# Keys turned for the outer products by a transposing DMA instead of TensorE, in a linear-attention and decision-tree layer on one core

## The chip, the cores and the metric

One core of a Trainium2 chip runs the whole layer. The metric is the device time of one execution in microseconds (us), lower is better. The kernel is written instruction by instruction for five engines that run at the same time and meet only at semaphores: TensorE (PE, with its weight loads as PEld), VectorE (DVE), ScalarE (ACT), GpSimd (POOL) and the queue that issues DMAs (SP). Each engine takes its instructions in the order in which they are written.

## The reference, cut to what matters

x is 4 x 2048 x 256 in float32. It is normalised by row (xn), and two branches are added to x:

```
Q = elu(xn @ Wq + bq) + 1      K = elu(xn @ Wk + bk) + 1      V = xn @ Wv + bv      # 16 heads of 64
KV[t] = KV[t-1] + K[t]^T V[t]          Ks[t] = Ks[t-1] + K[t]                       # causal, per head
attn  = (Q[t] KV[t]) / (Q[t] . Ks[t] + 1e-6) @ Wo + bo
gate  = sigmoid((xn @ tree_Wq^T) @ routers^T)                 # 255 nodes of a binary tree of depth 8
leaf  = product of gate or 1 - gate along each of 256 paths
out   = x + attn + (leaf @ leaf_values) @ Wout^T + Wout_b
```

## The kernel before

The 8192 tokens are 16 blocks of 512. In a block the 16 heads are taken two at a time, so a block has 8 units, p = 0 to 7, and the kernel 128 (n = 8 g + p). A unit takes its pair of heads in 8 chunks of 64 tokens: the products inside a chunk go through a masked matrix of scores, what came before goes through a running sum of outer products K^T V, kept as `snaps` (one after each chunk) and `state` (from block to block). V has a column of ones, which gives the denominator.

Precision comes from split operands: a float32 operand is held as a high part and a low part of TensorE's fast type, and a product is three passes (high by high, high by low, low by high). A projection of 256 inputs is therefore 6 matmuls of 512 columns. The high part is a copy by ScalarE (`high`, `high_of_output`), the low part a subtraction by VectorE (`low`, `low_of_output`).

PSUM is eight banks: two for outer products, and six that are filled and drained by turns, W0 and W1 (`w_pair`), S0 and S1 (`s_pair`), O0 and O1 (`o_pair`). A "fill" is a group of matmuls into one of the six; its drain frees the bank. S0 and S1 also hold the scores, O0 and O1 the outputs.

One unit n on TensorE:
- `tiled(n)`: the outputs of unit n from the state (`from_state`), the outer products of unit n + 1 (`outer_products_when_ready`; they need the keys by tokens, `k_tok`), the scores of unit n + 1 (`scores_when_ready`), the outputs of unit n from its masked scores (`from_chunk`). The scores wait until the queries of unit n + 1 are drained, and until S0 and S1 are: S1's last fill is the unit's "tail".
- the fills of `unit_fills(g, p)` (line 27), in that order: a head in W1 (V1 at p = 0, a transposed xn (`xT`) of the next block at p = 1, 2, transposed leaves at 3, 4, gates at 5, 6), the keys of unit n + 2 in W0, the queries of unit n + 2 in S0, the tail in S1 (a quarter of the values, at p = 0 to 6), the keys of unit n + 2 turned (`kT`, line 702: four 128x128 transposes, features by tokens into tokens by features), and the outputs of unit n turned (`oT`, line 709). At p = 7 there are the two halves of the block's result, `y`, instead of head and tail (60 matmuls each), and `kT` stands between them.

The other engines follow the same list. ScalarE (line 470): `copy_scores(n + 1)`, then by kind: `exponential` for K and Q (a Relu, line 407, and an Exp, line 410, on 128x512), `high` for xT and leaf, Tanh for gates, `copy_keys` for kT (line 420, PSUM to `k_tok`), `high_of_output` for oT (line 430). VectorE (line 617): `carry(n + 1)`, seven or eight dependent sums of outer products (line 585), `norm(n)`, then by kind: `phi` for K and Q (line 520), `low`, `values` (line 529), `low_of_output` (line 544). At p = 2 and 6 `values_first` puts the values ahead of the queries' phi. GpSimd (line 371): the mask of unit n + 1 (line 329), at p = 1 the residual (line 337), at p = 7 the eight levels of the next block's tree (lines 345 to 362), at p = 0 the inverse deviation. SP (line 284): the load of x two blocks ahead, and the two stores of a block's result.

`kT` and `qT` have two buffers each, by p % 2; `k_tok` has one.

Of the kernel before, what the change touches and what calls it, by code (L numbers as in the profile page):

```python
# [7 lines left out]
F32 = mybir.dt.float32  # L8
F32R = mybir.dt.float32r

P = 128
# [15 lines left out]
def unit_fills(g, p, blocks):  # L27

    n = g * PAIRS + p
    ahead = divmod(n + 2, PAIRS) if n + 2 < blocks * PAIRS else None  # L30
    more = g + 1 < blocks
    head, tail = [], []
    if p == 0:
        head, tail = [("V1", 0, g)], [("V1", 1, g)]
    if p in (1, 2):
        tail = [("V1", p + 1, g)]
        if more:
            head = [("xT", p - 1, g + 1)]
    if p in (3, 4):
        head = [("leaf", p - 3, g)]  # L40
        if more:
            tail = [("V0", p - 3, g + 1)]
    if p in (5, 6) and more:
        head, tail = [("gate", p - 5, g + 1)], [("V0", p - 3, g + 1)]

    fills = [(name, W1) for name in head]
    if ahead:
        fills += [(("K", ahead[1], ahead[0]), W0), (("Q", ahead[1], ahead[0]), S0)]
    fills += [(name, S1) for name in tail]
    if p == PAIRS - 1:  # L50

        fills += [(("oT", p, g), W1), (("y", 0, g), O1)]
    if ahead:
        fills.append((("kT", ahead[1], ahead[0]), W0))
    fills.append((("y", 1, g), S1) if p == PAIRS - 1 else (("oT", p, g), W1))
    return fills
# [4 lines left out]
         (("gate", 0, 0), S0), (("gate", 1, 0), S1), (("kT", 0, 0), W0), (("K", 1, 0), W0), (("Q", 1, 0), W1),  # L61
         (("kT", 1, 0), W0)]


def attention_and_tree_layer(nc, x, Wq, bq, Wk, bk, Wv, bv, Wo, bo,
# [45 lines left out]
    with ExitStack() as ctx:  # L111
        def sb(name, shape, dt=F32):
            return ctx.enter_context(nc.sbuf_tensor(name, shape, dt))

        def sem(name):
            return ctx.enter_context(nc.semaphore(name))
# [66 lines left out]
        tree_cols = [xn[:, 0:2].rearrange("p c n -> p (c n)"), xn[:, 2:4].rearrange("p c n -> p (c n)"),  # L183
                     k_tok[:, :, :].rearrange("p c n -> p (c n)")]
        leafvT, woutT, routersT = [t.rearrange("p (t n) -> p t n", t=2) for t in tree_cols]
# [39 lines left out]
        a_masked = sem("a_masked")  # L225
        kv_filled = sem("kv_filled")
        sum_ready = sem("sum_ready")
        o_begun = sem("o_begun")
# [28 lines left out]
        def _(sp):  # L257
# [25 lines left out]

            for g in range(BLOCKS):
                if g + 2 < BLOCKS:
                    sp.wait_ge(x_consumed, g + 1)
                    sp.dma_start(x_in[:, g % 2], x_rows[g + 2]).then_inc(x_loaded[g % 2], 16)
                for i in range(2):
                    name = ("y", i, g)
                    sp.wait_ge(drained[bank_of[name]], count_of[name])  # L290
                    sp.dma_start(out_rows[g, :, 2 * i:2 * i + 2, :],
                                 y_buf[:, 2 * i:2 * i + 2, :]).then_inc(y_stored, 16)
            sp.wait_ge(y_stored, 32 * BLOCKS)

        @block.gpsimd
        def _(pool):
# [67 lines left out]
            FIRST_LEVELS = {0: range(0, 5), 1: range(5, 7), 2: range(7, depth)}  # L364

            mask(0)
            gates(0)
            pool.wait_ge(leaf_step, 1)  # L370
            for n in range(UNITS):
                g, p = divmod(n, PAIRS)
                if p == 0 and g + 1 < BLOCKS:
                    inverse_deviation(g + 1)
                    pool.wait_ge(rstd_ready, 2 * g + 4)
                if n + 1 < UNITS:
                    mask(n + 1)
                if p == 1:
# [12 lines left out]
        @block.scalar  # L391
        def _(act):
# [25 lines left out]
            def copy_keys(name):  # L418
                act.wait_ge(filled[bank_of[name]], count_of[name])
                act.activation(k_tok[:, :, :].rearrange("p c n -> p (c n)"), psum_of(name), ACT.Copy)\  # L420
                   .then_inc(drained[bank_of[name]], 1)

            def high_of_output(name):
# [43 lines left out]
            exponential(("Q", 1, 0))  # L467
            copy_keys(("kT", 1, 0))

            for n in range(UNITS):  # L470
                if n + 1 < UNITS:
                    copy_scores(n + 1)
                for name, _ in unit_fills(n // PAIRS, n % PAIRS, BLOCKS):
                    kind, i, g = name
                    if kind in "KQ":
                        exponential(name)
                    elif kind == "oT":
                        high_of_output(name)
                    elif kind == "kT":
                        copy_keys(name)  # L480
                    elif kind == "xT":
                        high(name, xnT[:, g % 2, 0, i])
                    elif kind == "leaf":
                        high(name, leafT[:, 0, i])
                    elif kind == "gate":
                        half_gates(name)

        @block.vector
        def _(dve):
# [25 lines left out]
            def phi(name):  # L515
                kind, p, _ = name
                slot, dst = (0, kT) if kind == "K" else (1, qT)
                col = p + (PAIRS if kind == "K" else 0)
                dve.wait_ge(exp_ready, exp_count[name])
                dve.scalar_tensor_tensor(out=dst[:, p % 2], in0=psum_of(name), scalar=bias_one[:, col:col + 1],  # L520
                                         in1=ex[:, slot], op0=ALU.add, op1=ALU.max)\
                   .then_inc(drained[bank_of[name]], 1)
# [91 lines left out]
            carry(0)  # L614
            phi(("Q", 1, 0))

            for n in range(UNITS):
# [25 lines left out]
        def _(pe):  # L643
# [7 lines left out]

            def split_product(dst, lhs, rhs, tiles):
                steps = [s for t in range(tiles) for s in passes(lambda a, t=t: lhs(a, t), lambda a, t=t: rhs(a, t))]
                for i, (l, r) in enumerate(steps):
                    last = pe.matmul(dst, l, r, start=i == 0, stop=i == len(steps) - 1)  # L655
                return last
# [15 lines left out]

            def fill(name):
                kind, i, g = name
# [3 lines left out]
                if kind in "KQ":  # L678
                    wt = wk if kind == "K" else wq
                    last = split_product(dst, lambda a, t: wt[:, a, t, i * P:(i + 1) * P],  # L680
                                         lambda a, t: xnT[:, g % 2, a, t], KT_)
                elif kind in ("V0", "V1"):
                    half, n = int(kind[1]), 2 * HALF * D
                    last = split_product(dst, lambda a, t: xnT[:, g % 2, a, t, i * P:(i + 1) * P],
                                         lambda a, t: wv[:, a, t, half * n:(half + 1) * n], KT_)
                elif kind in ("xT", "leaf"):
# [13 lines left out]
                elif kind == "kT":  # L700
                    for c in range(CH):
                        last = pe.transpose(dst[:, c * P:(c + 1) * P], kT[:, i % 2, c * P:(c + 1) * P], ident[:, :])  # L702
# [172 lines left out]
            until_drained(("K", 1, 0))  # L875
            fill(("kT", 1, 0))
            until(split_lo_pool, len(LO_POOL))
            until(split_lo, len(LO_VECTOR))

            for n in range(UNITS):  # L880
                tiled(n)
                fills = unit_fills(n // PAIRS, n % PAIRS, BLOCKS)

                first_by_vector = fills[0][0][0] in ("V1", "xT", "leaf")
                for name, bank in fills:
# [15 lines left out]
                    if kind == "kT":  # L901
                        until_drained(("K", i, g))
                    fill(name)

# [24 lines left out]
```

## Time and profile before

| | |
|---|---|
| median of 3 runs | 1276.48 us (1273.93 to 1276.64) |
| the profiled execution | 1273.15 us, of which the trace's span is 1271.4 us |
| TensorE busy | 1244.6 us, 98% of the span (weight loads, beside it, 1105.0) |
| VectorE | 810.3 us, 64% |
| ScalarE | 622.4 us, 49% |
| GpSimd | 374.3 us, 29% |
| granted TensorE clock | 0.997 of full speed (2.4 GHz) |
| DMA | 25.91 MB in 21597 packets, 20 GB/s on average |

In the profile a line such as `676.80 0.75 DVE L520 ...` is an instruction (or a run of like ones, x6) with its start and its duration in us, the engine, the line of the kernel, the tile written, the tiles read and the shape; in brackets is how long the engine had been idle and what released it. TensorE's instructions overlap: the pitch from the start of one group to the start of the next is what a group costs, and the duration of one is longer than its share.

### The profile page before, as it was taken

How to read it: one execution, taken by the hardware profiler on the slowest of the kernel's cores; microseconds unless marked ns; L12 is line 12 of the kernel's file. 1: busy time of each engine (PE TensorE's matmuls, PEld its weight loads, DVE VectorE, ACT ScalarE, POOL GpSimd, SP SyncE). 2: the span in 40 equal slices, each digit the busy share in tenths (PEclk: the TensorE clock that was granted, in tenths of full speed). 3: DMA queues.
4: the chain of work that ended last, by engine and by line, in shares of the span. 5: the costliest groups of instructions: out<-in, count | busy, mean ns of one | idle time of the engine just before them, and what ended most of it. 6: DMA issues, size and time to landing. Idle time of an engine off the chain costs nothing.

```text
span 1271.4 us, 48688 instructions
## 1 busy us (share of the span) xinstructions
PE 1244.6 (98%) x22173; PEld 1105.0 (87%) x22173; DVE 810.3 (64%) x2186; ACT 622.4 (49%) x1007; POOL 374.3 (29%) x590
## 2 busy tenths in 40 slices
PE   5899999999999999999999999999999999999997
PEld 5789888898988989889898988989889898898986
DVE  4675766757576574765757666575765758657473
ACT  4563654536446363653636445364553636536361
POOL 3424232132421413223142321324214132231320
PEclk9899999999999999999999999999999999999999
DMA  6000001000000000001000010000000000000000
GB/s 223 19 3 19 19 2 35 3 18 20 10 28 3 19 19 10 28 3 36 2 19 19 3 35 3 19 20 10 28 3 19 19 18 20 2 19 3 19 3 18
DMA packets 21597, 25.91 MB, mean 20 GB/s; under 512 B 1025, under 2 KB 19728, under 8 KB 21392
## 3 DMA queue, kind: packets, MB, share of 16 engines
q1 hardware_dynamic: 21392, 22.82, 5.5%
q8 instruction: 173, 2.83, 0.9%
q14 instruction: 32, 0.26, 0.1%
HBM read 14.43 MB, written 8.39 MB: 18 GB/s over the span
## 4 chain that ended last, share of the span: by engine, by line
PE 97%; DVE 1%; ACT 1%; DMA 1%; SPq 0%; issue 0%; DVEq 0%
PE s_pair L655 25%; PE w_pair L655 20%; PE o_pair L667 9%; PE s_pair L667 9%; PE o_pair L765 6%; PE kv_pair L740 5%; PE o_pair L779 5%; PE s_pair L729 5%; PE w_pair L709 4%; PE w_pair L702 4%; PE w_pair L689 3%; DMA ffn_tok<-in_L_ffn_Wout_w_dram 1%; DVE snaps L585 0%; SPq L267 0%; PE o_pair L655 0%; ACT ex L407 0%
## 5 line engine op out<-in xcount | busy, mean ns | idle before, releaser
L329 POOL TENSOR_SCALAR_AFFINE_SELECT aT<-aT 64x512 f32<-64x512 f32 x256 | 167.6, 655 | 833.0 <-ACT aT L434 824.7
L655 PE MATMUL w_pair<-xnT,wk 128*128 128x512 f32 x768 | 205.7, 403 | 0.7 <-ACT k_tok L420 0.7
L655 PE MATMUL s_pair<-xnT,wq 128*128 128x512 f32 x756 | 194.0, 392 | 0.0
L434 ACT ACTIVATE aT<-s_pair 128x512 f32<-128x512 f32 x128 | 76.4, 597 | 238.3 <-PE s_pair L729 238.3
L585 DVE TENSOR_TENSOR snaps<-kv_pair,snaps 128x65 f32<-128x65 f32 x768 | 173.3, 226 | 26.4
L520 DVE SCALAR_TENSOR_TENSOR kT<-w_pair,bias_one,ex 128x512 f32<-128x512 f32 x128 | 96.2, 751 | 122.7 <-ACT ex L410 122.6
L655 PEld LDWEIGHTS s_pair<-xnT,wq 128*128 128x128 f32 x756 | 142.1, 188 | 31.4
L655 PE MATMUL s_pair<-wv,xnT 128*128 128x512 f32 x648 | 168.7, 395 | 0.0
L410 ACT ACTIVATE ex<-ex 128x512 f32<-128x512 f32 x256 | 161.8, 632 | 8.1
L407 ACT ACTIVATE ex<-w_pair,neg_bias 128x512 f32<-128x512 f32 x130 | 89.5, 689 | 148.5 <-PE w_pair L655 148.5
L655 PEld LDWEIGHTS w_pair<-xnT,wk 128*128 128x128 f32 x768 | 136.1, 188 | 26.6 <-ACT k_tok L420 1.0
L655 PEld LDWEIGHTS s_pair<-wv,xnT 128*128 128x128 f32 x648 | 121.6, 188 | 28.6
L420 ACT ACTIVATE k_tok<-w_pair 128x512 f32<-128x512 f32 x128 | 76.4, 597 | 143.0 <-PE w_pair L702 143.0
L520 DVE SCALAR_TENSOR_TENSOR qT<-s_pair,bias_one,ex 128x512 f32<-128x512 f32 x126 | 94.3, 748 | 59.6 <-ACT ex L410 59.6
L765 PE MATMUL o_pair<-snaps,qT 64*64 64x65 f32 x3584 | 112.2, 225 | 3.5 <-DVE state L585 3.5
L544 DVE TENSOR_TENSOR oT<-w_pair,oT 128x512 fp32r<-128x512 f32 x128 | 88.3, 690 | 27.4 <-ACT oT L430 27.4
L667 PE MATMUL o_pair<-wo,oT 128*128 128x256 f32 x768 | 94.7, 279 | 0.0
L667 PE MATMUL s_pair<-wo,oT 128*128 128x256 f32 x768 | 94.7, 279 | 0.0
L667 PEld LDWEIGHTS o_pair<-wo,oT 128*128 128x128 f32 x768 | 91.9, 188 | 0.0
L667 PEld LDWEIGHTS s_pair<-wo,oT 128*128 128x128 f32 x768 | 91.9, 188 | 0.0
L562 DVE TENSOR_TENSOR o_tok<-o_pair,rden 128x512 f32<-128x512 f32 x128 | 88.5, 691 | 4.4
L765 PEld LDWEIGHTS o_pair<-snaps,qT 64*64 64x64 f32 x3584 | 83.6, 135 | 8.7 <-issue 8.4
(105 smaller groups left out, 1953.7 us busy)
## 6 DMA issues: line engine op xcount, KB each, us to landing
x_in<-in_L_attn_x_dram SPq DMA_DIRECT2D x16, 512.0 KB, 3.9
out_dram<-y_buf SPq DMA_DIRECT2D x32, 256.0 KB, 2.1
stage<-in_L_attn_Wv_dram SPq DMA_DIRECT2D x2, 512.0 KB, 8.0
stage<-in_L_attn_Wk_dram SPq DMA_DIRECT2D x2, 512.0 KB, 9.6
stage<-in_L_attn_Wq_dram SPq DMA_DIRECT2D x2, 512.0 KB, 10.8
stage<-in_L_attn_Wo_dram SPq DMA_DIRECT2D x2, 512.0 KB, 9.1
bv_all<-in_L_attn_bv_dram SPq DMA_DIRECT2D x1, 512.0 KB, 8.6
ffn_tok<-in_L_ffn_Wq_dram SPq DMA_DIRECT2D x1, 256.0 KB
```

Of the source, the lines that this page charges most:

```text
L329: pool.affine_select(out=part, in_=part, compare_op=ALU.is_ge, fill=0.0, base=0, pattern=[[0, 2 * CH], [1, D]], channel_multiplier=-1).the ...
L407: act.activation(ex[:, slot], psum_of(name), ACT.Relu, scale=-1.0, bias=neg_bias[:, col:col + 1])\
L410: act.activation(ex[:, slot], ex[:, slot], ACT.Exp, scale=-1.0).then_inc(exp_ready, 1)
L420: act.activation(k_tok[:, :, :].rearrange("p c n -> p (c n)"), psum_of(name), ACT.Copy)\
L434: act.activation(aT[:, n % 2].rearrange("p h c q -> p h (c q)"), s_pair[:, :, 0:CH * D], ACT.Copy).then_inc(s_copied, 1)
L520: dve.scalar_tensor_tensor(out=dst[:, p % 2], in0=psum_of(name), scalar=bias_one[:, col:col + 1], in1=ex[:, slot], op0=ALU.add, op1=ALU.max)\
L544: dve.tensor_tensor(oT[:, 1, p], psum_of(name), oT[:, 0, p].bitcast(F32), ALU.subtract)\
L562: dve.tensor_tensor(o_tok[:, :, :, :].rearrange("p b t (h e) -> p b (t h) e", e=D), v[:, :, :, 0:D], rden[:, :, :].unsqueeze(3).to_broadca ...
L585: dve.tensor_tensor(dst, added, so_far, ALU.add).then_inc(sum_ready, 1)
L655: last = pe.matmul(dst, l, r, start=i == 0, stop=i == len(steps) - 1)
L667: last = pe.matmul(dst[:, (c % 2) * hid:(c % 2 + 1) * hid], oT[:, a, t, cols] if t < PAIRS else leafT[:, a, t - PAIRS, cols], wo[:, b, t] ...
L765: last = pe.matmul(output_at(t, h, a), qT[rows_of(h), p % 2, t * P + a * D:t * P + (a + 1) * D], before, start=turn == 0 and half not in b ...
```

## The change

- Order: the keys are filled first in each unit, ahead of the head, and three units ahead (n + 3) instead of two. The queries stay two ahead.
- The fill `kT` and its copy are gone, except for the first two units. In their place, for each unit m from 2 on: GpSimd (`take_apart`) reads the float32 keys as pairs of 16-bit words and writes the words into two planes, `k_planes` (128 x 2 x 512); SP (`turn_keys`) issues one transposing DMA from the planes to `k_turned` (128 x 8 x 128, 16 bits); ScalarE (`put_together`), ahead of the queries' exponential, copies the turned words back interleaved into `k_tok`.
- The waits go with it: the planes are free when the DMA before has landed, `k_turned` when ScalarE has put the previous keys together, `k_tok` when the outer products before have run. On TensorE, `masked` and `whole` wait for GpSimd's mask before the last matmul of the queries' fill, and for the keys put together before the last matmul of the tail.
- SP's order: the two stores of block g come at p = 0 of the next block, ahead of that unit's DMA, and the load of x at p = 2.
- At the end of a unit the order is now `oT`, after the tail; at p = 7, `oT`, then both halves of `y`.

```diff
@@ def unit_fills(g, p, blocks):
-    ahead = divmod(n + 2, PAIRS) if n + 2 < blocks * PAIRS else None
+    keys = divmod(n + 3, PAIRS) if n + 3 < blocks * PAIRS else None
+    queries = divmod(n + 2, PAIRS) if n + 2 < blocks * PAIRS else None
...
-    fills = [(name, W1) for name in head]
-    if ahead:
-        fills += [(("K", ahead[1], ahead[0]), W0), (("Q", ahead[1], ahead[0]), S0)]
+    fills = [(("K", keys[1], keys[0]), W0)] if keys else []
+    fills += [(name, W1) for name in head]
+    if queries:
+        fills.append((("Q", queries[1], queries[0]), S0))
     fills += [(name, S1) for name in tail]
+    fills.append((("oT", p, g), W1))
     if p == PAIRS - 1:
-        fills += [(("oT", p, g), W1), (("y", 0, g), O1)]
-    if ahead:
-        fills.append((("kT", ahead[1], ahead[0]), W0))
-    fills.append((("y", 1, g), S1) if p == PAIRS - 1 else (("oT", p, g), W1))
+        fills += [(("y", 0, g), O1), (("y", 1, g), S1)]
@@ buffers
+        k_planes = sb("k_planes", [P, 2, TOK], U16)
+        k_turned = sb("k_turned", [P, 2 * CH, P], U16)
@@ SP
-            for g in range(BLOCKS):
-                if g + 2 < BLOCKS:
-                    sp.wait_ge(x_consumed, g + 1)
-                    sp.dma_start(x_in[:, g % 2], x_rows[g + 2]).then_inc(x_loaded[g % 2], 16)
+            def turn_keys(m):
+                sp.wait_ge(k_apart, m - 1)
+                if m > 2:
+                    sp.wait_ge(k_whole, m - 2)
+                sp.dma_start_transpose(k_turned[:, :, :], k_planes[:, :, :].rearrange("p s t -> p (s t)"))\
+                  .then_inc(k_turned_in, 16)
...
+            turn_keys(2)
+            for n in range(UNITS):
+                g, p = divmod(n, PAIRS)
+                if p == 0 and g:
+                    store(g - 1)
+                if n + 3 < UNITS:
+                    turn_keys(n + 3)
+                if p == 2 and g + 2 < BLOCKS:
+                    sp.wait_ge(x_consumed, g + 1)
+                    sp.dma_start(x_in[:, g % 2], x_rows[g + 2]).then_inc(x_loaded[g % 2], 16)
@@ GpSimd (after the mask of unit n + 1, for unit n + 3)
+            def take_apart(m):
+                g, p = divmod(m, PAIRS)
+                pool.wait_ge(drained[bank_of["K", p, g]], count_of["K", p, g])
+                if m > 2:
+                    pool.wait_ge(k_turned_in, 16 * (m - 2))
+                pool.tensor_copy(k_planes[:, :, :], kT[:, m % 2].bitcast(U16).rearrange("p (t s) -> p s t", s=2))\
+                    .then_inc(k_apart, 1)
@@ ScalarE (before the queries' exponential)
+            def put_together(m):
+                act.wait_ge(k_turned_in, 16 * (m - 1))
+                act.wait_ge(kv_filled, m)
+                act.activation(k_tok[:, :, :].rearrange("p c f -> p (c f)").bitcast(U16)
+                               .rearrange("p (n s) -> p s n", s=2),
+                               k_turned[:, :, :].rearrange("p (s c) f -> p s (c f)", s=2), ACT.Copy).then_inc(k_whole, 1)
...
                     if kind in "KQ":
+                        if kind == "Q":
+                            put_together(n + 2)
                         exponential(name)
@@ TensorE
-                until_drained(("kT", p, g))
+                if n < 2:
+                    until_drained(("kT", p, g))
+                else:
+                    until(k_whole, n - 1)
...
-                        if c == 1 and g * PAIRS + i + 1 < UNITS:
-                            until(a_masked, 2 * (g * PAIRS + i) + 4)
...
+                def masked():
+                    if n + 1 < UNITS:
+                        until(a_masked, 2 * n + 4)
+                def whole():
+                    if n + 2 < UNITS:
+                        until(k_whole, n + 1)
...
-                    fill(name)
+                    fill(name, masked if kind == "Q" else whole if bank == S1 and kind != "y" else None)
+                    if kind == "y" and i == 0:
+                        whole()
+                masked()
+                whole()
```

## Rows read from the trace of the kernel before

**Rows 1.** The page's chain that ended last: shares of the span by engine

```profile
PE 97%; DVE 1%; ACT 1%; DMA 1%; SPq 0%; issue 0%; DVEq 0%
```

**Rows 2.** Stretches, p = 7, 0, 1: length, then each engine's busy us and count

```profile
641.28:661.19 19.91, 19.91 (x269) 19.15 (x268) 8.35 (x25) 5.08 (x9) 11.06 (x21) 1.00 0.05 15
661.19:669.84 8.65, 8.65 (x158) 7.32 (x157) 6.90 (x20) 3.56 (x6) 1.32 (x2) 1.00 0.09 32
669.84:677.58 7.74, 7.74 (x156) 6.67 (x155) 6.06 (x17) 4.93 (x9) 3.73 (x3) 1.00 0.01 4
```

**Rows 3.** Timeline of the unit p = 1: start, duration, engine, line, what

```profile
670.80 0.13 PEld L729 LDWEIGHTS s_pair<-qT,kT 64*64 64x64 f32 x1
...
671.95 0.66 PE L689 MATMUL w_pair<-ident,xn 128*128 128x128 f32 x4
...
675.41 0.69 ACT L407 ACTIVATE ex<-s_pair,neg_bias 128x512 f32<-128x512 f32 x1
...
676.13 0.63 ACT L410 ACTIVATE ex<-ex 128x512 f32<-128x512 f32 x1
...
676.61 0.60 PE L702 MATMUL w_pair<-ident,kT 128*128 128x128 f32 x4
676.80 0.75 DVE L520 SCALAR_TENSOR_TENSOR qT<-s_pair,bias_one,ex 128x512 f32<-128x512 f32 x1 [0.62 <-ACT ex L410]
...
677.05 0.60 PE L709 MATMUL w_pair<-ident,o_tok 128*128 128x128 f32 x4
...
677.47 0.68 DVE L529 TENSOR_TENSOR v_aug<-s_pair,bv_all 128x512 f32<-128x512 f32 x1
...
678.54 0.13 PEld L729 LDWEIGHTS s_pair<-qT,kT 64*64 64x64 f32 x1
```

**Rows 4.** Timeline of the unit p = 7, whose keys are filled first

```profile
643.39 1.66 PE L655 MATMUL w_pair<-xnT,wk 128*128 128x512 f32 x6
...
645.09 0.69 ACT L407 ACTIVATE ex<-w_pair,neg_bias 128x512 f32<-128x512 f32 x1 [1.43 <-PE w_pair L655]
...
647.19 0.63 ACT L410 ACTIVATE ex<-ex 128x512 f32<-128x512 f32 x1
647.29 2.87 PEld L667 LDWEIGHTS o_pair<-wo,oT 128*128 128x128 f32 x24
...
647.72 0.58 ACT L430 ACTIVATE oT<-w_pair 128x512 fp32r<-128x512 f32 x1
...
648.52 0.68 DVE L544 TENSOR_TENSOR oT<-w_pair,oT 128x512 fp32r<-128x512 f32 x1
```

**Rows 5.** Timeline of the unit p = 6, values ahead of the queries' phi

```profile
632.57 0.13 PEld L765 LDWEIGHTS o_pair<-state,qT 64*64 64x64 f32 x1 [0.17 <-issue]
...
640.51 0.69 DVE L529 TENSOR_TENSOR v_aug<-s_pair,bv_all 128x512 f32<-128x512 f32 x1 [0.64 <-PE s_pair L655]
...
641.12 0.74 DVE L520 SCALAR_TENSOR_TENSOR qT<-s_pair,bias_one,ex 128x512 f32<-128x512 f32 x1
...
642.29 0.56 PEld L729 LDWEIGHTS s_pair<-qT,kT 64*64 64x64 f32 x32
```

**Rows 6.** Groups by line and shape: operations of 1024 columns, busy us, mean ns

```profile
L345 POOL TENSOR_SCALAR ffn_tok<-ffn_tok 128x1024 f32<-128x1024 f32 x16 | 17.6, 1102 | 1.4
...
L396 ACT ACTIVATE wv<-stage 128x1024 fp32r<-128x1024 f32 x2 | 2.1, 1050 | 0.0
```

**Rows 7.** DMA queues (packets, MB, share), then DMA issues (KB each, us to landing)

```profile
q1 hardware_dynamic: 21392, 22.82, 5.5%
...
x_in<-in_L_attn_x_dram SPq DMA_DIRECT2D x16, 512.0 KB, 3.9
out_dram<-y_buf SPq DMA_DIRECT2D x32, 256.0 KB, 2.1
stage<-in_L_attn_Wv_dram SPq DMA_DIRECT2D x2, 512.0 KB, 8.0
...
stage<-in_L_attn_Wq_dram SPq DMA_DIRECT2D x2, 512.0 KB, 10.8
```

More of the change, by code:

```diff
@@ L9 @@
 F32R = mybir.dt.float32r
+U16 = mybir.dt.uint16
 P = 128
@@ L226, in attention_and_tree_layer @@
         kv_filled = sem("kv_filled")
+        k_apart = sem("k_apart")
+        k_turned_in = sem("k_turned_in")
+        k_whole = sem("k_whole")
         sum_ready = sem("sum_ready")
@@ L292, in _ @@
                                  y_buf[:, 2 * i:2 * i + 2, :]).then_inc(y_stored, 16)
+            turn_keys(2)
[8 more added lines that the diff above has]
+                    sp.dma_start(x_in[:, g % 2], x_rows[g + 2]).then_inc(x_loaded[g % 2], 16)
+            store(BLOCKS - 1)
             sp.wait_ge(y_stored, 32 * BLOCKS)
@@ L370, in _ @@
             pool.wait_ge(leaf_step, 1)
+            take_apart(2)
             for n in range(UNITS):
@@ L377, in _ @@
                     mask(n + 1)
+                if n + 3 < UNITS:
+                    take_apart(n + 3)
                 if p == 1:
@@ L468, in _ @@
             copy_keys(("kT", 1, 0))
+            exponential(("K", 2, 0))
             for n in range(UNITS):
@@ L515, in phi @@
             def phi(name):
-                kind, p, _ = name
-                slot, dst = (0, kT) if kind == "K" else (1, qT)
+                kind, p, b = name
+                slot, dst = (0, kT[:, p % 2]) if kind == "K" else (1, qT[:, p % 2])
                 col = p + (PAIRS if kind == "K" else 0)
                 dve.wait_ge(exp_ready, exp_count[name])
-                dve.scalar_tensor_tensor(out=dst[:, p % 2], in0=psum_of(name), scalar=bias_one[:, col:col + 1],
+                dve.scalar_tensor_tensor(out=dst, in0=psum_of(name), scalar=bias_one[:, col:col + 1],
                                          in1=ex[:, slot], op0=ALU.add, op1=ALU.max)\
@@ L615, in _ @@
             phi(("Q", 1, 0))
+            phi(("K", 2, 0))
             for n in range(UNITS):
@@ L650, in until, with split_product @@
                     pe.wait_ge(signal, count)
-            def split_product(dst, lhs, rhs, tiles):
+            def split_product(dst, lhs, rhs, tiles, at_last=None):
                 steps = [s for t in range(tiles) for s in passes(lambda a, t=t: lhs(a, t), lambda a, t=t: rhs(a, t))]
                 for i, (l, r) in enumerate(steps):
+                    if at_last and i == len(steps) - 1:
+                        at_last()
                     last = pe.matmul(dst, l, r, start=i == 0, stop=i == len(steps) - 1)
@@ L671, in output_rows, with fill @@
                 return last
-            def fill(name):
+            def fill(name, at_last=None):
                 kind, i, g = name
@@ L684, in fill @@
                     last = split_product(dst, lambda a, t: xnT[:, g % 2, a, t, i * P:(i + 1) * P],
-                                         lambda a, t: wv[:, a, t, half * n:(half + 1) * n], KT_)
+                                         lambda a, t: wv[:, a, t, half * n:(half + 1) * n], KT_, at_last)
                 elif kind in ("xT", "leaf"):
@@ L701, in fill @@
                     for c in range(CH):
-                        last = pe.transpose(dst[:, c * P:(c + 1) * P], kT[:, i % 2, c * P:(c + 1) * P], ident[:, :])
+                        last = pe.transpose(dst[:, c * P:(c + 1) * P], kT[:, i, c * P:(c + 1) * P], ident[:, :])
                 elif kind == "oT":
                     for c in range(CH):
-                        if c == 1 and g * PAIRS + i + 1 < UNITS:
-                            until(a_masked, 2 * (g * PAIRS + i) + 4)
                         to = dst[:, c * P:(c + 1) * P].rearrange("p (a q) -> p a q", a=2)
@@ L876, in _ @@
             fill(("kT", 1, 0))
+            fill(("K", 2, 0))
             until(split_lo_pool, len(LO_POOL))
@@ L882, in _ @@
                 fills = unit_fills(n // PAIRS, n % PAIRS, BLOCKS)
-                first_by_vector = fills[0][0][0] in ("V1", "xT", "leaf")
+                first_by_vector = any(bank == W1 and name[0] in ("V1", "xT", "leaf") for name, bank in fills)
+                def masked():
[4 more added lines that the diff above has]
+                        until(k_whole, n + 1)
                 for name, bank in fills:
```

14 lines of the change are left out of this document (6 added, 8 removed).

## The prediction

> **What bounds the kernel now.** I read the chain of waits first: 97% of the span is TensorE running its own queue [rows 1]. Next the table by stretches: within a block of eight units TensorE is busy for every microsecond of the unit, whether that is the 19.91 us of p = 7, the 8.65 of p = 0 or the 7.74 of p = 1 and 2, at the full clock, while ScalarE is busy for 4.93 of 7.74 us and VectorE for 6.06 [rows 2]. So TensorE is the bound, but the other two are not idle bystanders. The timeline of the unit p = 1 shows how far behind TensorE they follow [rows 3]: TensorE starts the scores of the next unit at 678.54, and just before it VectorE finished phi of the queries (676.80 + 0.75 = 677.55) and then the values (677.47 + 0.68 = 678.15). The scores need both: the queries as an operand, and both S banks empty. The margin is 0.39 us. That margin decides this case.
>
> **What goes.** Four transposes of the keys per unit. Their price is the pitch from their first record to the first of the next group, 677.05 - 676.61 = 0.44 us [rows 3] (the mean of one record is longer, since records overlap). 126 times 0.44 is 55 us. ScalarE's copy of the turned keys out of PSUM goes as well (0.60 us, off the path). If nothing else became late, this would be the gain.
>
> **What comes, and what it costs.** (1) GpSimd splits the keys into planes, 128x1024 elements. The nearest row is its 128x1024 tensor_scalar, 1.10 us [rows 6]; two-byte elements at a stride could cost double, 2.2; I take 1.1. GpSimd is idle most of a unit; at p = 7 the tree's levels start some 3 us later, 11 us of work in a unit of 20, and nothing waits for them until p = 3. (2) ScalarE puts the halves together, again 1024 elements: its 128x1024 SBUF to SBUF copy takes 1.05 us [rows 6]. From below, a 512-column operation is 0.60; from above I see no reason for more than 1.3. I take 1.05. This stands before the queries' exponential in ScalarE's order. (3) The transposing DMA, 256 KB. No row shows one. From below the plain 256 KB store lands in 2.1 us. From above, the weight loads in a full queue land in 8.0 to 10.8 us [rows 7]. Between them: 21392 packets took 5.5% of 16 engines over 1271.4 us, so 52 ns each; the 512 KB load (1 KB packets, 32 to an engine) lands in 3.9 us, of which packets are 1.7 and 2.2 is fixed. If each of 128 partitions and 8 column blocks makes a packet, 64 come to an engine: 3.3 + 2.2 = 5.5 us, the value that I take.
>
> **Is the DMA hidden?** In unit p = 1 keys are filled first. Counting from the unit's start (669.84), the first fill starts at 2.11 (671.95 [rows 3]); a fill of keys in first place is ready for ScalarE 1.70 later (643.39 to 645.09 [rows 4]), so at 3.81; Relu and Exp take 1.35 (675.41 to 676.76), phi 0.75, ending at 5.95; planes to 7.1; SP issues. Putting together stands 5.55 into the next unit (below), 7.74 us or more later: 13.3. So 6.1 us are there for the DMA, and 5.5 just fits. The store of the output and x's load stand in the same queue, but one transfer per unit of 8 us leaves them room; the store at p = 0 is issued before this unit's keys exist.
>
> The Trainium skill disagrees with itself here. "VectorE: DVE Perf Modes", section "The three transpose paths", gives 1309 ns for a 128x128 block through the crossbar, eight of which would be an estimated 10.5 us and not fit; "DMA: Bandwidth & Descriptors" has 261 GB/s for transposes, an estimated 1.0 us of data for 256 KB, which would fit. No run here shows either yet.
>
> **What is late instead.** Before, ScalarE did the head fill's copy in its idle time ahead of the keys; now it comes behind the keys' exponential, and putting together behind that. Unit p = 1, from its start: keys' Relu 3.81; the next independent operation follows Exp 0.53 after its start (647.19 to 647.72 [rows 4], so operations overlap by 0.1), so at 3.81 + 0.72 + 0.53 = 5.06; the copy of xT, 0.60 with 0.1 overlapped, to 5.55; putting together, 0.95 net, to 6.50. The queries' Relu thus starts at 6.50 where it started at 5.57 (675.41). Exp ends at 7.85, phi runs from 7.89, the values follow 0.67 later (676.80 to 677.47) and end at 9.24. With 0.1 for the signal the next scores start at 9.34. TensorE would be there at 7.30 + 0.96 = 8.26. Before it was 8.70 (678.54). So p = 1 gets longer by 0.64 although TensorE has 0.44 less to do. After the first such unit this repeats, since keys are filled 1.15 us after the scores start, in either order.
> p = 3 and 4 have the same order (a leaf copy in xT's place): +0.64 each. At p = 2 the values precede the queries' phi, which ends at 8.64: scores at 8.74, +0.04.
> p = 5 and 6 are 8.71 long (632.57 to 641.28 [rows 2, 5]): their head, gates, takes about 1 us more, by which the queries come later too. In the old order the scores start 3.13 after the queries' Relu (678.54 - 675.41), so at p = 5, where they start at 9.73, Relu is at 6.60. Now gates' Tanh is at 5.2, putting together at 5.7, the queries at 6.64, and the scores 2.84 later (the values' end, 678.15 - 675.41, and 0.1), at 9.48: -0.25. p = 6: values ready at 7.95 (640.51 - 632.57 = 7.94 [rows 5]), phi 0.61 behind, scores at 9.41 instead of 9.72 (642.29 - 632.57): -0.31.
> p = 0: scores were at 8.65 + 0.96 = 9.61, so the queries' Relu at 6.48. ScalarE has no copy for the head here and is through with putting together at 6.1, so Relu stays where it is, and the scores come at 6.48 + 2.84 = 9.32: -0.29.
> p = 7: the queries wait 0.82 for putting together, so the low half of the last output, which ended at 649.21, ends at 650.03; its first reader is the 22nd of 24 weight loads that start at 647.29 at 0.117 each, 649.74 [rows 4]. A stall of 0.37 against 0.44 saved: -0.07.
> Sum of a block: -0.29 + 0.64 + 0.04 + 0.64 + 0.64 - 0.25 - 0.31 - 0.07 = +1.04; 15 blocks, +15.6. The last block has no values at p = 3 and 4, where the new chain costs 0.95 each, and smaller terms elsewhere: +1.9. At the start the third keys have no unit of lead: fill, exponentials, phi, planes, DMA, putting together are 1.7 + 1.35 + 0.75 + 1.1 + 5.5 + 1.05 = 11.5 us, from 1.4 before the first unit, needed at about 7.5 in it: +2.6. In all +20.1 on the profiled execution's 1273.15 us (span 1271.4 and 1.75 around it). The median is 3.3 above that execution: 1276.48 + 20.1 = 1296.6; rounded down a little for overlaps that I don't see, 1295.
>
> **Rivals.**
> A, the forecast: ScalarE's longer queue before the queries' exponential takes the gain back. 1295, its own range 1280 to 1312. Chance 0.53.
> B, faster: ScalarE has the room. Were putting together as cheap as a 512-column copy (0.60), queries start 0.45 earlier at p = 1 to 4 and p = 7: p = 1, 3, 4 cost +0.19 each, p = 2 gains 0.41, p = 7 0.44, p = 0, 5, 6 about 0.9 together: -1.2 a block, -17 in all with the ends, 1259. It decides below about 0.8 us for that operation. With all of it hidden the limit is -55, 1221. For it: ScalarE is busy for only 4.93 of 7.74 us [rows 2]. Against it: where its work stands, not how much it is, and the 1.05 us row. Chance 0.21.
> C, the ring: landing, putting together (1.05), next issue, landing; a unit can't be shorter than the DMA plus 1.25, since there is one buffer for planes and one for turned halves. It costs from 6.5 us on. At the 8.0 us of the load of Wv units take 9.25: p = 1 to 4 +1.5 each, p = 0 +0.6, p = 5 and 6 +0.54 each, so 7.7 a block, 16 blocks: 1400. Chance 0.17.
> D, the eight blocks go one after another: at the 10.8 us of Wq's load a unit takes 12.05, 27 us more in a block, 1710. Against it: that load waited behind others in its queue. Chance 0.09. (The Trainium skill's 1309 ns a block, in "VectorE: DVE Perf Modes", "The three transpose paths", would mean a rival of this kind.)
>
> **How the numbers follow.** A change under 0.2% (2.6 us) can't be told from none. Faster: B and a thin edge of A, 0.22. Same: where A and B meet, 0.07. Slower: A's rest, C, D, 0.71. The range: a tenth below, from B's faster half, and a tenth above, from C's upper part and D: 1245 to 1375.
>
> **What would show it.** In the profile after: no key transposes on TensorE; at p = 1, 3, 4 units of some 8.4 us with TensorE waiting for VectorE's values before the scores; p = 0, 5, 6 shorter by 0.3; the queries' Relu released by ScalarE itself and not by TensorE; putting together at 1.05 us; the transpose landing in under 6.1 us. Wrong if units 1, 3 and 4 are shorter than 7.7 us, or if ScalarE idles before putting together for a DMA.

## The result and the profile after

The change makes the kernel slower: 1307.59 us median (1304.73 to 1307.94, 4 runs) against 1276.56, a ratio of 1.0235 with a 95% interval of [1.0213, 1.0256]. Forecast were 1295 and a range of 1245 to 1375. The profiled execution took 1307.69 us, its span is 1306.0.

The page of the changed kernel: span, busy time by engine, then the chain that ended last, by engine and by line.

```profile
span 1306.0 us, 48282 instructions
...
PE 1244.0 (95%) x21669; PEld 1059.6 (81%) x21669; DVE 801.0 (61%) x2186; ACT 687.3 (53%) x1007; POOL 504.8 (39%) x716
...
PE 60%; ACT 25%; DVE 9%; issue 5%; DMA 1%; SPq 0%; POOL 0%; DVEq 0%; POOLq 0%
PE w_pair L705 20%; ACT k_tok L464 9%; PE s_pair L717 9%; ACT ex L444 8%; PE s_pair L705 8%; PE s_pair L778 5%; PE o_pair L717 5%; PE o_pair L828 5%; DVE qT L567 5%; ACT ex L447 5%; PE o_pair L814 3%; DVE v_aug L576 3%; PE kv_pair L789 3%; PE w_pair L758 2%; ACT leafT L437 1%
```

Where TensorE had 97% of the chain [rows 1], it has 60%, and ScalarE 25%. The largest of ScalarE's lines there is L464, the interleaving. TensorE's busy sum hardly fell (1244.6 to 1244.0 us), although 504 transposes are gone: without them and without the rest of the change it is 1194.7 (the floor below). The three largest groups of fills (w_pair<-xnT,wk; s_pair<-xnT,wq; s_pair<-wv,xnT) have the same counts as before and 32 us more of busy time, so the sum counts some waiting as work and does not show the loss.

The chain itself, in order of time, through the unit p = 1 (start, length, what):

```profile
686.99 0.53 PE s_pair L778 x30
...
688.05 1.60 PE w_pair L705 x6
689.64 0.02 issue
689.67 0.70 ACT ex L444
690.37 0.02 issue
690.39 0.02 ACT ex L447
690.41 0.51 issue
690.93 0.58 ACT xnT L437
691.51 1.26 ACT k_tok L464
692.77 0.54 ACT ex L444
693.31 0.02 issue
693.33 0.64 ACT ex L447
693.98 0.03 issue
694.00 0.75 DVE qT L567
694.75 0.61 DVE v_aug L576
695.36 0.04 issue
695.40 0.62 PE s_pair L778 x26
```

This is the forecast's queue, link by link: keys' fill, keys' Relu and Exp, the copy of xT, the interleaving, the queries' Relu and Exp, phi of the queries, the values, the scores. Before the change the queries' Relu started at 675.41 [rows 3], 0.04 us after the last matmul of its fill (673.84 + 1.53), with ScalarE done 0.02 us earlier:

```profile
673.84 1.53 PE L655 MATMUL s_pair<-xnT,wq 128*128 128x512 f32 x6
...
674.76 0.63 ACT L410 ACTIVATE ex<-ex 128x512 f32<-128x512 f32 x1
```

There the chain runs through TensorE alone; now the Relu has its fill ready and waits for ScalarE's own queue.

One unit goes another way. At p = 2 the chain leaves the interleaving for TensorE itself, in 15 of the 16 blocks: the last matmul of the tail has the new wait for the keys put together (`whole`).

```profile
700.02 1.27 ACT k_tok L464
701.29 0.04 issue
701.33 0.50 PE s_pair L705
```

The outer products, which read those keys, begin only at 702.62. No run moves this wait nearer to them.

The two new operations that matter, by line over the whole run (ns min/median/max), and the DMA's issue (median us to landing):

```profile
L464 ACT ACTIVATE k_tok<-k_turned x126: 1342/1364/1378, 52.2 to 1273.2; 128x1024 uint16<-128x1024 uint16 x126
```

```profile
L396 POOL COPY k_planes<-kT x126: 1037/1042/1045, 47.9 to 1267.9; 128x1024 uint16<-128x1024 uint16 x126
L296 SPq DMA_TRANSPOSE k_turned<-k_planes x126: 1232/1232/2453, 49.0 to 1269.0; - x126
```

```profile
k_turned<-k_planes SPq DMA_TRANSPOSE x126, 3.1
```

The interleaving takes 1.36 us where 1.05 was forecast. GpSimd's split takes 1.04 (1.1 forecast). The only wait that the profile puts to this DMA is that of the first interleaving, 1.2 us. Rivals C and D are out.

How long is a unit? Medians over the blocks of the time from one `copy_scores` of ScalarE to the next, read from the timelines (the columns on the right are experiments below):

| fills of unit | before | forecast | after | floor, no keys turned | straight copy | GpSimd interleaves |
|---|---|---|---|---|---|---|
| p = 0 | 8.78 | 8.49 | 8.34 | 8.35 | 8.33 | 8.33 |
| p = 1 | 7.74 | 8.38 | 8.50 | 7.33 | 8.24 | 7.38 |
| p = 2 | 7.74 | 7.78 | 7.95 | 7.41 | 7.67 | 7.46 |
| p = 3 | 7.73 | 8.37 | 8.49 | 7.31 | 8.22 | 7.38 |
| p = 4 | 7.74 | 8.38 | 8.51 | 7.33 | 8.25 | 7.39 |
| p = 5 | 8.77 | 8.52 | 8.67 | 8.30 | 8.39 | 8.37 |
| p = 6 | 8.71 | 8.40 | 8.41 | 8.39 | 8.40 | 8.45 |
| p = 7 | 19.83 | 19.76 | 19.97 | 19.37 | 19.70 | 19.36 |
| block | 77.04 | 78.08 | 78.84 | 73.79 | 77.20 | 74.12 |

The sign is as forecast in all units but p = 7, which got longer. A block costs 1.80 us more; over 15 blocks that is 27 of the 31. Of the profiled executions, whose spans differ by 34.6, the one after reaches its first copy of scores 3.7 us later (40.66 against 36.92). That is ahead of the first transposing DMA, and the experiments show that it does not belong to the change.

### The profile page after: what moved, and what is told of

The parts are those of the page before. It is cut to its first block, busy times and chain, and to the rows that moved or that the text cites. A ratio compares the mean times of both kernels' runs of the same rounds, so it can differ in the third digit from the quotient of the medians.

```text
span 1306.0 us, 48282 instructions
## 1 busy us (share of the span) xinstructions
PE 1244.0 (95%) x21669; PEld 1059.6 (81%) x21669; DVE 801.0 (61%) x2186; ACT 687.3 (53%) x1007; POOL 504.8 (39%) x716
## 2 busy tenths in 40 slices
DMA packets 154655, 58.94 MB, mean 45 GB/s; under 512 B 134082, under 2 KB 152785, under 8 KB 154449
## 3 DMA queue, kind: packets, MB, share of 16 engines
q1 hardware_dynamic: 154448, 55.86, 20.4%
HBM read 14.43 MB, written 8.39 MB: 17 GB/s over the span
## 4 chain that ended last, share of the span: by engine, by line
PE 60%; ACT 25%; DVE 9%; issue 5%; DMA 1%; SPq 0%; POOL 0%; DVEq 0%; POOLq 0%
PE w_pair L705 20%; ACT k_tok L464 9%; PE s_pair L717 9%; ACT ex L444 8%; PE s_pair L705 8%; PE s_pair L778 5%; PE o_pair L717 5%; PE o_pair L828 5%; DVE qT L567 5%; ACT ex L447 5%; PE o_pair L814 3%; DVE v_aug L576 3%; PE kv_pair L789 3%; PE w_pair L758 2%; ACT leafT L437 1%
## 5 line engine op out<-in xcount | busy, mean ns | idle before, releaser
L396 POOL COPY k_planes<-kT 128x1024 uint16<-128x1024 uint16 x126 | 131.1, 1041 | 282.2 <-issue 254.6
L705 PE MATMUL w_pair<-xnT,wk 128*128 128x512 f32 x768 | 213.0, 413 | 4.1 <-ACT k_tok L457 2.2
L705 PE MATMUL s_pair<-xnT,wq 128*128 128x512 f32 x756 | 201.9, 402 | 0.2 <-ACT aT L479 0.2
L705 PE MATMUL s_pair<-wv,xnT 128*128 128x512 f32 x648 | 185.1, 405 | 12.1 <-ACT k_tok L464 12.0
L464 ACT ACTIVATE k_tok<-k_turned 128x1024 uint16<-128x1024 uint16 x126 | 171.9, 1364 | 1.2 <-DMA k_turned<-k_planes 1.2
L705 PEld LDWEIGHTS s_pair<-xnT,wq 128*128 128x128 f32 x756 | 135.9, 189 | 25.8 <-POOL aT L353 0.6
L778 PE MATMUL s_pair<-qT,kT 64*64 64x64 f32 x4096 | 107.9, 223 | 17.1 <-DVE v_aug L576 12.5
L778 PEld LDWEIGHTS s_pair<-qT,kT 64*64 64x64 f32 x4096 | 85.5, 134 | 30.4 <-DVE v_aug L576 23.0
L717 PE MATMUL o_pair<-wo,oT 128*128 128x256 f32 x768 | 99.9, 283 | 4.7 <-DVE oT L591 4.7
L576 DVE TENSOR_TENSOR v_aug<-s_pair,bv_all 128x512 f32<-128x512 f32 x108 | 73.9, 684 | 45.6 <-PE s_pair L705 45.6
```

The lines of the kernel that those rows point to most:

```text
L396: pool.tensor_copy(k_planes[:, :, :], kT[:, m % 2].bitcast(U16).rearrange("p (t s) -> p s t", s=2))\
L464: act.activation(k_tok[:, :, :].rearrange("p c f -> p (c f)").bitcast(U16) .rearrange("p (n s) -> p s n", s=2), k_turned[:, :, :].rearrang ...
L576: dve.tensor_tensor(dst, psum_of(name).rearrange("p (h e) -> p h e", e=D), bv_all[:, half * n:(half + 1) * n].rearrange("p (h e) -> p h e" ...
L717: last = pe.matmul(dst[:, (c % 2) * hid:(c % 2 + 1) * hid], oT[:, a, t, cols] if t < PAIRS else leafT[:, a, t - PAIRS, cols], wo[:, b, t] ...
L778: last = pe.matmul(s_pair[rows_of(a), h, t * D:(t + 1) * D], kT[rows_of(h), p % 2, at], qT[rows_of(h), p % 2, at], start=True, stop=True)
```

## Experiments

All times are medians; ratios are to the kernel before on the same chip. My theory: the loss is ScalarE's queue ahead of the queries' exponential, by its place and its length. The rivals: the DMA or GpSimd disturb the other engines; the new order or the new waits cost by themselves.

**Floor.** What can be saved at most.

```diff
-    if ahead:
-        fills.append((("kT", ahead[1], ahead[0]), W0))     # in the kernel before; first two units keep theirs
```

> The kernel before, with the turning of the keys left out from the third unit on (no transposes, no copy; k_tok keeps old keys), so its time is that of what the change can save at most. Forecast of my theory: TensorE's 0.44 us per unit goes, but at p = 1, 3, 4 the values' drain (0.1 us of signal behind it) then holds the scores about 0.2 us, so -0.26 there and -0.3 to -0.44 elsewhere: 1233, with 1221 as the limit if nothing holds. Rival (the transposes were hidden in part): above 1250.

Measured 1225.44, ratio 0.9600 [0.9573, 0.9627], 8 us below the expected 1233. The transposes of the keys were worth 51 of the 55 us in the forecast: they were on the path, at 0.32 to 0.47 us a unit where 0.44 was forecast.

**No DMA, no split.**

```diff
-            turn_keys(2) ... turn_keys(n + 3)
-            take_apart(2) ... take_apart(n + 3)
+            pool.memset(k_turned[:, :, :], 0).then_inc(k_turned_in, 16)
-                act.wait_ge(k_turned_in, 16 * (m - 1))
+                act.wait_ge(k_turned_in, 16)
```

> The changed kernel without GpSimd's split and without the transposing DMA; ScalarE puts together the same zeros each time, at the same place (the keys by tokens are left out of the result). If ScalarE's order alone makes the loss, it stays at 1303 to 1308 (a start term of 1 to 3 us goes). If the DMA or GpSimd's second operation slow the others down, it falls: below 1290.

Measured 1301.66, ratio 1.0200 [1.0181, 1.0220], just below the expected range. The medians of its units are those of the changed kernel to within 0.02 us, p = 0 to 7 (8.33, 8.50, 7.94, 8.48, 8.51, 8.65, 8.41, 19.97). So 33 MB of transposing DMA and 131 us of GpSimd's split cost nothing in the loop. The 6 us are at the two ends: 3.0 before the first scores' copy (37.67 against 40.66), 1.0 in the first unit, 2.4 in units 4 and 5 of the last block.

The 3.0 are not the price of the DMA. The first transposing DMA is issued at 49.0, after that copy, and the eight kernels below that have the DMA and the split copy their first scores at 36.73 to 37.95: one profiled execution got through its first loads late.

The 2.4 hold two gaps of TensorE, 0.44 and 0.98 us, for which the profile shows no wait (`issue` in the brackets). Here the second, and the one at the same place in the kernel in which GpSimd interleaves:

```profile
1272.43 0.27 PE L778 MATMUL s_pair<-qT,kT 64*64 64x64 f32 x1 [0.98 <-issue]
```

```profile
1198.30 0.27 PE L777 MATMUL s_pair<-qT,kT 64*64 64x64 f32 x1 [1.23 <-issue]
```

Six kernels with the DMA (the changed one, read side, half, straight, and both with GpSimd) have gaps of 0.44 to 1.77 us at these two places, and each of the twelve ends within 0.3 us of the last packet of a transposing DMA (the one above at 1272.43, its last packet at 1272.24). Without the DMA there is none over 0.25 us; but three kernels with it (interleaving first, one column, values first) have none either. So a transposing DMA in flight goes with these gaps; what TensorE lacks in them is open.

**Interleaving first in the unit.**

```diff
                 if n + 1 < UNITS:
                     copy_scores(n + 1)
+                if n + 2 < UNITS:
+                    put_together(n + 2)
...
-                        if kind == "Q":
-                            put_together(n + 2)
```

> The changed kernel with one call moved: ScalarE puts the keys of unit n + 2 together right behind its copy of the scores, where it idled 1.43 us, instead of ahead of the queries' exponential. Theory (the place in ScalarE's queue, not its amount): the queries' Relu is again released by TensorE, units p = 1, 3, 4 take about 7.5 us, 1233 in all, as the kernel that turns no keys. Rival (ScalarE's operation is too long wherever it stands: 1.36 us against 1.43 idle): it pushes the keys' Relu, 1250 to 1275. Rival (contention by the DMA): above 1280.

Measured 1284.52, ratio 1.0060 [1.0037, 1.0082]. The theory's 1233 failed. The number lies in the band of the last rival, but not for its reason: the run without DMA shows no contention in the loop. The kernel's chain through p = 1 and 2 shows why:

```profile
683.15 1.05 POOL k_planes L396
684.20 0.02 issue
684.22 4.51 DMA k_turned<-k_planes
688.73 0.02 issue
688.75 1.37 ACT k_tok L464
690.12 0.53 ACT ex L444
690.66 0.02 issue
690.68 0.64 ACT ex L447
691.32 0.03 issue
691.35 0.76 DVE kT L566
...
692.22 1.04 POOL k_planes L396
```

From the issue to the release of the copy the DMA takes 4.51 us (1.23 of it the issue itself), and a slot at 2.4 us into the next unit is too early for keys whose planes were ready at 7.1 in this one. ScalarE then waits, and with it the keys' Relu. This is a ring, but not rival C's (landing, putting together, next issue): it runs from the landing through the interleaving, the keys' Relu and Exp, phi and the split to the next issue, 9.07 us from one split to the next (683.15 to 692.22), and it is closed by moving the slot forward. ScalarE waited 98.7 us for the DMA in 80 units. At p = 0 and p = 1 the units (8.33 and 7.39) are within 0.06 of the floor. My expectation had left the landing out of its own account.

**Three lengths of the same operation.** By the read side, half of it, and straight.

```diff
-   out p (n s) -> p s n ,  in  p (s c) f -> p s (c f)     # as changed: reads in order, writes every second word
+   out p (n s) -> p n s ,  in  p (s c) f -> p (c f) s     # gather: reads alternately, writes in order
+   ... [:, 1]  on both                                    # half: 512 words, written at a stride
+   out in order, in the high plane twice, in order        # straight
```

> The changed kernel with the interleaving on the read side: ScalarE writes k_tok in order and reads the two turned planes alternately, where it read in order and wrote every second 16-bit word. If the 0.31 us above the float32 copy of 1024 columns (1.05) come from writing words at a stride, the operation falls to about 1.05, each 0.1 us of it is worth 0.1 at p = 1, 2, 3, 4 and 7, so -25: 1283. If they come from 16-bit data or from reading at a stride, it stays at 1.36 or more and the time at 1307 or above.

Measured 1291.53, ratio 1.0115 [1.0091, 1.0140]; the operation takes 1.174. Not the 1.05 asked about, but shorter, and 16 us for 0.19 us.

> The changed kernel with half of the interleaving left out: ScalarE copies 512 of the 1024 columns (high words alone). The operation falls from 1.36 to about 0.78. Theory: p = 1, 3, 4, 7 get 0.58 shorter, p = 2 0.54 (then TensorE binds), p = 5 0.26: 3.1 a block, 1257. If the loss were a fixed cost of the new waits and not the length of this operation: above 1290.

Measured 1255.41, ratio 0.9833 [0.9812, 0.9854]; the operation takes 0.778. Forecast 1257.

> The changed kernel with ScalarE's operation made straight: it writes k_tok in order and reads the plane of the high words twice, in order (1024 16-bit elements as before; the low words are left out). Interleaving by the write side took 1.36, by the read side 1.17. If strides are the whole surplus over the float32 copy, it takes 1.05 and the kernel 1291.5 - 0.12 * 5 * 16 = 1282. If 16-bit data has a cost of its own, it stays at 1.17 and 1291.

Measured 1277.64 (forecast 1282), ratio 1.0015 [1.0005, 1.0026]; the operation takes 1.047. 16-bit elements have no cost of their own here; strides are the whole surplus, 0.13 on the read side and 0.32 on the write side. Their rows, gather, half, straight:

```profile
L464 ACT ACTIVATE k_tok<-k_turned x126: 1162/1174/1192, 49.5 to 1257.6; 128x1024 uint16<-128x1024 uint16 x126
```

```profile
L464 ACT ACTIVATE k_tok<-k_turned x126: 761/778/791, 48.5 to 1220.6; 128x512 uint16<-128x512 uint16 x126
```

```profile
L464 ACT ACTIVATE k_tok<-k_turned x126: 1041/1047/1057, 48.5 to 1244.0; 128x1024 uint16<-128x1024 uint16 x126
```

Against the changed kernel the three save 16, 52 and 30 us for 0.19, 0.59 and 0.32 us of this operation: 84 to 95 us per us. A part of that is the changed kernel's late start in the profiled executions, 2.7 to 3.7 us. In the loop alone they save 0.83, 3.21 and 1.64 us a block, which is 70 to 88 us per us over 16 blocks. The straight copy is 0.26 to 0.28 us shorter a unit at p = 1 to 5 and 7, and equal at p = 0 and 6: the operation counts in six of a block's eight units.

**No interleaving.** A copy of one column in its place.

```diff
-                act.activation(k_tok ..., k_turned ..., ACT.Copy).then_inc(k_whole, 1)
+                act.activation(stub[:, m % 2:m % 2 + 1], k_turned[:, 0, 0:1], ACT.Copy).then_inc(k_whole, 1)
```

> The changed kernel with the interleaving left out (a copy of one column stands in its place, k_tok keeps old keys); split and DMA stay. Theory: 1230 to 1240, units as with GpSimd's copy. If the DMA or GpSimd's split cost anything in the loop, it is above 1250.

Measured 1233.51, ratio 0.9667 [0.9641, 0.9693]. The rest of the change, DMA, split, order and waits, is 8 us above the floor. One ScalarE operation is worth 74 us.

**Values before the queries' phi.** The end of the queue, on VectorE.

```diff
-                if p not in (2, PAIRS - 2):
+                if p == PAIRS - 1:
                     return fills
```

> The changed kernel with VectorE's values ahead of the queries' phi in all units but p = 7 (before only at p = 2 and 6). Theory: at p = 1, 3, 4 the scores then wait for phi, which ends 0.6 earlier than the values did, and p = 5 becomes like p = 6: -0.6 three times and -0.25, 16 blocks, -33: 1275. Rival (the scores wait for the queries alone, and the values are not on the path): no change, 1307.

Measured 1271.22, ratio 0.9954 [0.9938, 0.9970]: -36 against -33 forecast. p = 1, 3, 4 fall from 8.50 to 7.92, p = 5 to 8.34. The values' drain behind phi was on the path. But the time came out for another reason than the theory's: phi does not hold the scores now. In 61 of the 64 units p = 1 to 4 the chain leaves the interleaving for the last matmul of the tail, the wait that p = 2 had in the changed kernel:

```profile
671.05 1.28 ACT k_tok L464
672.33 0.04 issue
672.38 0.50 PE s_pair L705
```

So the agreement of -36 with -33 is in part luck. Of the 36, moreover, 3.6 are the changed kernel's late start (40.66 against 37.02).

**The order alone.** In the kernel before, TensorE turns the keys.

```diff
-    fills = [(name, W1) for name in head]
-    if ahead: fills += [K, Q]
+    fills = [K] if ahead else []
+    fills += [(name, W1) for name in head]
+    if ahead: fills += [Q]
```

> The kernel before with the order alone changed: the keys' fill ahead of the head's, still two units ahead, TensorE still turns the keys. Theory: the head's copy moves behind the keys' exponential (to 5.55 in the unit), but the queries' Relu is due at 5.57 to 5.6, so nothing is late: 1276, within 3 us. If the new order by itself costs, p = 1, 3, 4 grow by 0.1 or more and it is above 1281.

Measured 1277.04, ratio 1.0013 [0.9995, 1.0031]. p = 1 to 4 grow by 0.04 to 0.06, p = 5 falls by 0.04: nothing that the total shows.

**GpSimd interleaves.** What the others point to: keep the DMA, take the operation off the queue that is full at that point. GpSimd copies it between its mask and its split.

```diff
+            def put_together(m):                       # GpSimd
+                pool.wait_ge(k_turned_in, 16 * (m - 1))
+                pool.wait_ge(kv_filled, m)
+                pool.tensor_copy(<k_tok as before>, <k_turned as before>).then_inc(k_whole, 1)
...
                     mask(n + 1)
+                if n + 2 < UNITS:
+                    put_together(n + 2)
                 if n + 3 < UNITS:
                     take_apart(n + 3)
```

> The changed kernel with one operation moved to another engine: GpSimd, not ScalarE, interleaves the turned halves, between its mask and its split. Everything else of the change stays. Theory (ScalarE's queue ahead of the queries' exponential makes the whole loss): the queries' Relu comes back to 5.57 in the unit, p = 1, 3, 4 take about 7.4 us, the block is that of the kernel that turns no keys plus nothing: 1228 to 1235, faster than both kernels. Rival (DMA ring: landing 4.5 us behind the planes, then a copy and the next split on GpSimd): the copy would have to start later than 5 us into the unit and hold up TensorE before the tail's last matmul: 1250 or more.

Measured 1233.46 us (1232.52 to 1234.92), ratio 0.9661 [0.9637, 0.9685]. It beats both kernels, by 43 and by 74 us, and equals the kernel without any interleaving. That equality is a sum of two differences: at p = 7 this kernel is 0.42 shorter (19.36 against 19.78), and its last block is 3.5 longer, 2.7 of it in two gaps of the kind shown above (1.51 and 1.23). Its chain is TensorE's again:

```profile
PE 95%; DMA 1%; POOL 1%; DVE 1%; ACT 1%; issue 1%; SPq 0%; POOLq 0%; DVEq 0%
```

and the unit p = 2 of its timeline shows three engines side by side (start, length, engine, line; in brackets the idle time before and what ended it):

```profile
657.96 0.69 ACT L453 ACTIVATE ex<-w_pair,neg_bias 128x512 f32<-128x512 f32 x1 [1.46 <-PE w_pair L704]
...
658.36 1.36 POOL L405 COPY k_tok<-k_turned 128x1024 uint16<-128x1024 uint16 x1 [0.35 <-POOL aT L353]
658.68 0.63 ACT L456 ACTIVATE ex<-ex 128x512 f32<-128x512 f32 x1
659.22 0.58 ACT L446 ACTIVATE xnT<-w_pair 128x512 fp32r<-128x512 f32 x1
659.35 0.75 DVE L566 SCALAR_TENSOR_TENSOR kT<-w_pair,bias_one,ex 128x512 f32<-128x512 f32 x1 [0.64 <-ACT ex L456]
...
659.79 0.69 ACT L453 ACTIVATE ex<-s_pair,neg_bias 128x512 f32<-128x512 f32 x1
...
660.16 1.04 POOL L396 COPY k_planes<-kT 128x1024 uint16<-128x1024 uint16 x1 [0.44 <-DVE kT L566]
```

The queries' Relu starts 1.83 us after the keys' (659.79 - 657.96); by the pieces of the changed kernel's chain it was 3.10 (692.77 - 689.67).

**The same by the read side.**

```diff
-   out p (n s) -> p s n ,  in  p (s c) f -> p s (c f)
+   out p (n s) -> p n s ,  in  p (s c) f -> p (c f) s
```

> GpSimd interleaves, now by the read side. GpSimd waits for most of a unit, so its duration (1.36 by the write side) is off the path: no change against the write side's 1233.5, within 2 us, whatever the operation takes. If GpSimd's length were on the path (its copy holds the split of the next keys), a shorter one would gain 2 us or more, a longer one lose them.

Measured 1233.25, ratio 0.9658 [0.9632, 0.9684]; GpSimd's copy falls from 1.362 to 1.163 us and the time does not move. The same 0.2 us that ScalarE paid with 16 us is free on GpSimd.

## Why the prediction was right, and where it was not

**TensorE's gain** was put at 0.44 us a unit, 55 us as a limit: the floor shows 51.

**The DMA hidden** with 5.5 us in a budget of 6.1: right, with 4.5 us measured from issue to release. It moves 1056 packets (154655 - 21597, over 126), about the 1024 that I counted, but each took 24 ns and not 52: (20.4% of 16 x 1306.0 - 5.5% of 16 x 1271.4) / 133058. Of the Trainium skill's two figures, the 1309 ns a block ("VectorE: DVE Perf Modes", "The three transpose paths") does not add up over blocks here: eight would be an estimated 10.5 us and took 4.5 with everything. The Trainium skill's other figure, 261 GB/s ("DMA: Bandwidth & Descriptors", "Latency and other measured facts"), would be an estimated 1.0 us of data; the packets' 66 x 24 ns on each engine are 1.6.

**The mechanism, rival A's,** was right: place and length of ScalarE's work ahead of the queries' exponential, by units as forecast, but for p = 2. There the forecast had the queries' phi hold the scores, and the chain has TensorE's new wait for the keys put together, at the tail's last matmul, which the prediction gives no price. The move to GpSimd and the copy of one column both give back all 74 us, and leaving out DMA and split gives back none of it in the loop.

**The term that was mis-sized** is "from above I see no reason for more than 1.3. I take 1.05" for putting together. The float32 copy that I took it from writes and reads in order, this one writes every second word, and took 1.36. The straight copy, at 1.047, is the kernel that my sum describes: it came out at 1277.64, so the missing 0.32 us are 30 us (25 of them in 15 blocks of 1.64, and 3.7 in the profiled executions' starts).

**A second error, the other way,** hid more than half of the first. With 1.05 the sum was +20.1; the straight copy measures +1.5. A block costs 0.16 more and not 1.04. The units p = 1, 3 and 4 were forecast 0.13 to 0.15 too long each, p = 0 0.16, p = 2 0.11 and p = 5 0.13. Two reasons show in the rows. I gave 0.1 us to the signal from VectorE to TensorE, where the chain has 0.04. And the scores do not wait as a whole: four of their 32 records stand at 694.81, behind the queries' phi, and 0.59 ahead of the rest, which the values' drain released. How much each is worth was not measured. 15 blocks of 0.88 are 13 us of the 18.6. Of the rest, the first and last units hold some 3: I had put them at +4.5, and the traces have the straight copy's at about +1. The remainder is the way of counting: by medians the straight copy is 1.5 above the kernel before, by the profiled executions 4.3 (1277.47 against 1273.15). So 1295 came nearer to 1307.6 than its parts deserve: the sign rested on the right mechanism, but a kernel with the interleaving at its forecast length would have been at no change or barely above it (1.0015 [1.0005, 1.0026]). That the change is clearly slower, as forecast, is owed to the mis-sized term: in that the forecast was lucky.

**p = 7** was to gain 0.07 and lost 0.14. The place is the forecast's: the 22nd weight load of the first output half waits for the last output's low half.

```profile
744.71 0.68 DVE L591 TENSOR_TENSOR oT<-w_pair,oT 128x512 fp32r<-128x512 f32 x1
...
745.44 0.41 PEld L717 LDWEIGHTS o_pair<-wo,oT 128*128 128x128 f32 x3 [0.53 <-DVE oT L591]
```

0.53 us of stall where 0.37 was forecast. The longer interleaving accounts for it: with the straight copy p = 7 is at 19.70, 0.13 below before.

**Rival B** had its condition right in kind (faster if the operation is short enough), but not its price: at 0.778 the kernel is already at 1255, where 1259 was forecast for 0.60 and no change for about 0.8. The break-even is later than I said: 1.047 us still cost 1.5 us in all, at some 90 per us that puts it near 1.03. It is the same second error. What B did not consider is another engine.

## What to carry to other kernels

Before giving an engine a new operation, write down its instructions between the fill that releases it and the last drain that the bound engine waits for; an engine at 49% of the span can have no room at that one place, and here each microsecond put there cost 70 to 90. An engine that is idle there can take the part that moves data from SBUF to SBUF, as GpSimd did. Price a copy by a row with the same strides, not only the same element count. A forecast names each new wait and where it stands; the one at the tail's last matmul held p = 2. The transposing DMA two units ahead of its use cost nothing in this loop, but its landing is part of every new slot's account.

## What the runs showed of the hardware

- A 128x1024 copy of 16-bit words, ScalarE: 1.047 us in order, 1.174 reading alternately from two planes, 1.364 writing every second word (1.357 without any DMA). GpSimd: 1.163 and 1.362 for the latter two, and 1.04 when it reads at a stride of two words and writes in order (the split). The write side at a stride cost both engines the same.
- A 256 KB transposing DMA inside SBUF: 1.23 us of issue, landing 3.1 us by the issue table, 4.51 from the start of the issue to the release of its reader. 126 of them, 15% of the DMA engines' time (20.4% with the loads and stores, which alone are 5.3% without the DMA), changed the median of no unit by more than 0.02 us. In the last block, in six kernels, TensorE stood still for 0.44 to 1.77 us until such a DMA's packets had ended; why is open.
